# Retention in 128x32 column tiles accumulated in PSUM, and the score mask in four 64x64 tiles a slot

## The reference, cut to what matters

```python
# retention, 16 heads of 8 channels
q = l2_normalize(xn @ qw.T);  k = l2_normalize(xn @ kw.T);  v = xn @ vw.T
sim = einsum('bhnd,bhmd->bhnm', qh, kh) * scale
sim = sim * dmask            # gamma[h] ** (n - m) where n >= m, else 0
yh = einsum('bhnm,bhmd->bhnd', sim, vh)
x = x + (yh @ ow.T + ob)
...
# local attention, window 64
sim = where((i < j) | (i > j + WINDOW) | (j == -1), -big, sim)
attn = softmax(sim)
```

## Time and profile before

| what | us |
|---|---|
| time, median of 3 runs | 1068.89 (1068.8 to 1069.12) |
| time of the profiled execution | 1067.32 |
| span from its first to its last instruction | 1065.5 |
| outside the span (1067.32 - 1065.5) | 1.8 |

### The profile page before, as it was taken

One profiled execution on the slowest core, in us unless ns is written; L12 is line 12 of the kernel. 1 busy time (PEld: TensorE's weight loads), 2 busy tenths in 40 slices (PEclk: granted clock), 3 DMA queues, 4 the chain that ended last, 5 costly groups with the idle time before them and its releaser, 6 DMA issues.

```text
span 1065.5 us, 22792 instructions
## 1 busy us (share of the span) xinstructions
PE 964.0 (90%) x8404; PEld 660.6 (62%) x8404; DVE 752.1 (71%) x1225; ACT 693.1 (65%) x1347; POOL 619.8 (58%) x474
## 2 busy tenths in 40 slices
PE   1679899999999999999999969999999999999876
PEld 1347676685676766857767655756565656565552
DVE  5766676676767766767677676678787979696833
ACT  1354765847757658477576657777777768786643
POOL 4576566655755666558566655665665757575600
PEclk9989999999999999999999989999999999999997
DMA  9000000000000000000000000000000000000000
GB/s 293 1 1 1 1 2 2 2 1 0 0 1 0 0 0 0 0 0 0 0 0 0 1 1 1 2 2 21 0 20 0 20 0 20 0 20 0 21 21 10
DMA packets 20404, 12.31 MB, mean 12 GB/s; under 512 B 4578, under 2 KB 19596, under 8 KB 20236
## 3 DMA queue, kind: packets, MB, share of 16 engines
q1 hardware_dynamic: 15108, 10.49, 3.2%
q10 hardware_dynamic: 5256, 1.28, 0.6%
HBM read 9.67 MB, written 2.10 MB: 11 GB/s over the span
## 4 chain that ended last, share of the span: by engine, by line
PE 57%; DVE 15%; ACT 10%; POOL 8%; issue 7%; DMA 1%; DVEq 1%; ACTq 0%; SPq 0%; POOLq 0%
PE pQK L1140 6%; PE pS L1043 4%; PE pT L1054 4%; PE pS L1069 4%; PE pM L1086 4%; PE pT L1016 3%; PE pM L1210 3%; PE pS L1251 3%; PE pV L1106 3%; DVE m L720 3%; DVE xa L890 3%; PE pQK L1285 2%; DVE ss L710 2%; PE pS L1030 2%; PE pT L1242 2%
## 5 line engine op out<-in xcount | busy, mean ns | idle before, releaser
L367 POOL TENSOR_TENSOR rn<-rn,half_neg 128x16 f32<-128x16 f32 x64 | 187.5, 2929 | 5.3
L380 POOL TENSOR_TENSOR m<-m 128x1024 f32<-128x1024 f32 x64 | 150.9, 2358 | 0.0
L365 POOL TENSOR_SCALAR rn<-ss 128x16 f32<-128x16 f32 x64 | 16.5, 258 | 219.9 <-DVE ss L710 218.6
L730 DVE TENSOR_REDUCE mx<-pS 128x8 f32<-128x1024 f32 x64 | 78.1, 1220 | 74.4 <-PE pS L1043 74.4
L387 POOL TENSOR_TENSOR qkn<-m,rn 128x1024 f32<-128x1024 f32 x64 | 123.7, 1933 | 6.1 <-POOL m L380 2.0
L1140 PE MATMUL pQK<-wqkv,hT 128*128 128x512 f32 x256 | 124.2, 608 | 1.9 <-DVE m L720 1.9
L511 ACT ACTIVATE kT<-pT 128x512 f32<-128x512 f32 x64 | 38.0, 595 | 94.3 <-PE pT L1016 93.8
L551 ACT ACTIVATE sq<-pQK 128x1024 f32<-128x1024 f32 x64 | 65.4, 1021 | 29.9 <-PE pQK L1140 29.9
L710 DVE TENSOR_REDUCE ss<-sq 128x16 f32<-128x1024 f32 x64 | 77.4, 1210 | 7.0 <-ACT sq L551 6.9
L535 ACT ACTIVATE prT<-pT 128x1024 f32<-128x1024 f32 x64 | 65.4, 1022 | 25.5 <-PE pT L1054 24.4
L732 DVE TENSOR_TENSOR pr<-pS,mx 128x1024 f32<-128x1024 f32 x64 | 78.3, 1224 | 2.2
(11 more groups left out here) (172 smaller groups left out, 2356.8 us busy)
## 6 DMA issues: line engine op xcount, KB each, us to landing
x<-in_L_attn_x SPq DMA_DIRECT2D x4, 512.0 KB, 8.2
xs<-in_L_attn_x SPq DMA_DIRECT2D x8, 256.0 KB, 2.8
out<-aqkT SPq DMA_DIRECT2D x8, 256.0 KB, 2.3
wqkv<-in_L_ffn_wqkv SPq DMA_DIRECT2D x2, 768.0 KB, 10.4
tab<-in_k_tab SPq DMA_DIRECT2D x1, 1024.0 KB, 10.8
w<-in_L_ffn_w SPq DMA_DIRECT2D x2, 341.0 KB, 10.5
wo<-in_L_ffn_wo SPq DMA_DIRECT2D x2, 256.0 KB
cst<-in_k_cst ACTq DMA_DIRECT2D x1, 404.5 KB, 3.6
```

Source lines behind the costliest of these rows:

```text
L367: eng.tensor_tensor(rn[:, k % 2, :], rn[:, k % 2, :], half_neg[:, 0:2 * H], ALU.pow).then_inc(S["rn_done"], 1)
L380: eng.tensor_tensor(m1[:, k % 2, :], m1[:, k % 2, :], m2[:, k % 2, :], ALU.add).then_inc(S["add_done"], 1)
L730: eng.tensor_reduce(mx[:, :], sc, AX.X, ALU.max).then_inc(S["mx_done"], 1)
```

## The change

1. **Values** (`pe_block_values`): 16 matmuls of 128x32 weights by 32 columns a block, one for each chunk and residue j of the head in its group, each into a column tile of 32 PSUM partitions. They read the input itself, so the fourfold copy `xa4` goes. DVE spreads the 128 columns over 512 while it masks (L846 before; the output stays 512 elements).
2. **Sums** (`pe_block_sums`): ACT copies v into `avm` in 4 instructions with 32, 64, 96 and 128 rows; 4 matmuls of 128x32 weights by 128 columns, in four column tiles, give all chunks at once. DVE masks 128 columns in place of 512.
3. **State**: it is no longer added by DVE. PE adds it in PSUM, and POOL updates it once a step for the four blocks, at the end of its retention (`pool_state`).
4. **Output** (`pe_block_output`): 4 matmuls by 128 columns (state), 12 by 32 columns (sums of earlier chunks), 16 by 32 columns (`vx` with `sm`), all in column tiles of one bank `pY`, which holds four blocks. ACT copies it out once a step in place of 16 times.
5. **Order**: the projections run two blocks ahead in two banks (`qkv_banks`), and the scores of a block come after the next block's transposes.
6. **Mask** (`pe_scores`): four matmuls of 64x64 weights by 512 columns, one for each quarter of the array, in place of two of 128x128.

```diff
-            mask = mask16[:, 0 if is_first(step) else 1, :].unsqueeze(1).broadcast_to([P, 4, P])
-            for g in range(2):
-                eng.matmul(pS[:, g * 512:(g + 1) * 512], mask16[:, 2, :], mask, start=True, stop=False,
-                           skip_group_check=True)
+            for w in range(2):
+                for g in range(2):
+                    r = slice(64 * g, 64 * g + 64)
+                    kind = 2 if w else (0 if is_first(step) else 1)
+                    mask = mask16[r, kind * P:(kind + 1) * P].unsqueeze(1).broadcast_to([64, 4, P])
+                    eng.matmul(pS[64 * w:64 * w + 64, g * 512:(g + 1) * 512], mask16[r, 3 * P:3 * P + WIN], mask,
+                               start=True, stop=False, skip_group_check=True)
...
+        def pe_block_values(eng, t, b):
+            need(eng, A["vx"], 4 * t + b)
+            for c_ in range(NBL):
+                for j in range(NG):
+                    mm = eng.matmul(pT[BL * j:BL * j + BL, c_ * BL:(c_ + 1) * BL], xa[:, b, c_ * BL:(c_ + 1) * BL],
+                                    value_weights[:, :, j, :], start=True, stop=True)
+            mm.then_inc(A["vx_mm"], 1)
...
+        def pe_block_sums(eng, t, b):
+            if b == 0:
+                eng.wait_ge(LS["o_done"], 4 * t + 1)
+            need(eng, A["kvm"], 4 * t + b)
+            for g in range(NG):
+                cols = slice(BL * g, BL * g + BL)
+                mm = eng.matmul(pS[cols, 0:P].rearrange("p (c n) -> p c n", c=NBL), aqk[:, b % 2, 1, cols],
+                                avm[:, b % 2, :, cols], start=True, stop=True)
+            mm.then_inc(A["kv_mm"], 1)
...
+        def pe_block_output(eng, t, b):
+            n = 4 * t + b
+            need(eng, A["state"], t)
+            for g in range(NG):
+                rows = slice(BL * g, BL * g + BL)
+                eng.matmul(pY[rows, b * P:(b + 1) * P].rearrange("p (c n) -> p c n", c=NBL), state[:, b, :],
+                           qx[:, b % 2, :, g, :], start=True, stop=False, skip_group_check=True)
+            eng.wait_ge(A["kvm"], n + 1)
+            for c_ in range(1, NBL):
+                for g in range(NG):
+                    rows, col0 = slice(BL * g, BL * g + BL), b * P + c_ * BL
+                    eng.matmul(pY[rows, col0:col0 + BL], before[:, b, c_ - 1, :], qx[:, b % 2, c_, g, :], start=False,
+                               stop=False, skip_group_check=True)
+            eng.wait_ge(A["vx"], n + 1)
+            eng.wait_ge(A["sm"], n + 1)
+            for c_ in range(NBL):
+                for g in range(NG):
+                    rows, col0 = slice(BL * g, BL * g + BL), b * P + c_ * BL
+                    mm = eng.matmul(pY[rows, col0:col0 + BL], vx[:, b % 2, c_, rows], sm[:, b % 2, c_, g, :],
+                                    start=False, stop=True, skip_group_check=True)
+            mm.then_inc(A["y_mm"], 1)
...
         def dve_retention(eng, t, old):
             for k in range(NB + 1):
+                if k > 0:
+                    dve_block_scores(eng, t, k - 1)
                 if k < NB:
-                    if k < NB - 1:
-                        dve_retention_qk(eng, t, k + 1)
                     eng.wait_ge(A["vx_mm"], n + 1)
...
+                if k == 0:
+                    dve_retention_qk(eng, t, 1)
+                if k + 2 < NB:
+                    dve_retention_qk(eng, t, k + 2)
+                if k == NB - 1 and old:
+                    dve_ln(eng, old)
...
             need(eng, A["kv_mm"], n - 1)
-            eng.activation(av[:, b % 2, :], pV[:, 2 * P:3 * P], ACT.Copy).then_inc(A["v"], 1)
+            for c_ in range(NBL):
+                rows = slice(0, (c_ + 1) * BL)
+                copied = eng.activation(avm[rows, b % 2, c_, :], bank[rows, 2 * P:3 * P], ACT.Copy)
+            copied.then_inc(A["v"], 1)
...
+        def pool_state(eng, t):
+            eng.wait_ge(A["y_mm"], 4 * t + 4)
+            eng.tensor_tensor(state[:, :, :], state[:, :, :], state_decay.unsqueeze(2).broadcast_to([P, NB, BL]),
+                              ALU.mult).then_inc(A["faded"], 1)
+            eng.wait_ge(A["faded"], t + 1)
+            eng.tensor_tensor(state[:, :, :], state[:, :, :], before[:, :, NBL - 1, :], ALU.add).then_inc(A["state"], 1)
```

More of the change, by code:

```diff
@@ L51 @@
 C_END = C_SD + 1
+MASK_END = 3 * P + WIN
 def constants():
@@ L88, in constants @@
     before = (i[:WIN, None] <= i[None, :WIN])
+    first = np.concatenate([own, np.zeros_like(before)], 1)
     even = np.concatenate([own, before], 1)
     odd = np.concatenate([before, own], 1)
[L91 to L95, removed]
+    mask = np.where(np.concatenate([first, even, odd], 1), 0.0, MASKED).astype(f)
+    mask = np.concatenate([mask, np.eye(WIN, dtype=f)], 1)
+    mask = np.concatenate([mask, mask], 0)
     return cst, np.ascontiguousarray(tab), np.ascontiguousarray(mask)
@@ L600, in act_retention_project @@
             n = 4 * t + b
[L601 to L606, removed]
+            bank = qkv_banks[b % 2]
             eng.wait_ge(A["qkv_mm"], n + 1)
@@ L629, in act_retention @@
                         act_shift_residual(eng, old)
[L630 to L637, removed]
+                if k + 2 < NB:
+                    act_retention_project(eng, t, k + 2)
+            eng.wait_ge(A["y_mm"], 4 * t + 4)
+            eng.activation(ayT, pY, ACT.Copy).then_inc(A["yt"], 1)
         def act_block_ffn(eng, t):
@@ L872, in dve_block_scores @@
             eng.wait_ge(A["st_mm"], n + 1)
+            need(eng, A["y_mm"], n - 1)
             eng.tensor_tensor(sm[:, b % 2, :, :, :],
@@ L1218, in pe_retention_project @@
                 eng.wait_ge(LS["v_ev"], 2 * (4 * t + 4))
-            need(eng, A["qk"], 2 * n)
-            eng.matmul(pV[:, 0:3 * P], xa[:, b, :], aT[:, 0:3, :], start=True, stop=True).then_inc(A["qkv_mm"], 1)
+            need(eng, A["qk"], 2 * (n - 1))
+            eng.matmul(qkv_banks[b % 2][:, 0:3 * P], xa[:, b, :], aT[:, 0:3, :], start=True,
+                       stop=True).then_inc(A["qkv_mm"], 1)
         def pe_retention(eng, t, old):
@@ L1254, in pe_retention @@
-                if k == NB - 1:
-                    if old:
-                        eng.wait_ge(A["t_ev"], 4 * t + 4)
-                        pe_ln(eng, old)
-                    pe_block_scores(eng, t, k)
-                if k > 0:
-                    b = k - 1
-                    n = 4 * t + b
-                    eng.wait_ge(A["sm"], n + 1)
-                    eng.wait_ge(A["before"], n + 1)
-                    need(eng, A["yt"], NG * (n - 1))
-                    for c_ in range(NBL):
-                        cols = slice(512 + c_ * P, 512 + (c_ + 1) * P)
-                        eng.matmul(y_banks[b % 2][:, cols], vx[:, b % 2, c_, :], sm[:, b % 2, c_, :, :], start=True, stop=False)
-                        mm = eng.matmul(y_banks[b % 2][:, cols], before[:, b % 2, c_ - 1, :] if c_ else state[:, b, :],
-                                        qx[:, b % 2, c_, :, :], start=False, stop=True)
-                    mm.then_inc(A["y_mm"], 1)
@@ L1272, in pe_retention @@
-                if k < NB - 1:
-                    pe_block_scores(eng, t, k)
+                if k == 0:
+                    pe_retention_project(eng, t, 1)
+                if k > 0:
+                    pe_block_scores(eng, t, k - 1)
+                if k + 2 < NB:
+                    pe_retention_project(eng, t, k + 2)
+                if k == NB - 1 and old:
+                    eng.wait_ge(A["t_ev"], 4 * t + 4)
+                    pe_ln(eng, old)
+                if k < NB:
+                    pe_block_values(eng, t, k)
+                    pe_block_sums(eng, t, k)
```

139 lines of the change are left out of this document (59 added, 80 removed).

## The result

The changed kernel takes 1042.71 us (median), the kernel before took 1068.85 us on the same chip: 0.9747 of it, with a 95% interval of 0.9733 to 0.976. It is faster, by 26.1 us where I had forecast 66; 1042.7 lies 2.7 us above my range. (One further execution of the changed kernel took 1561.88 us at a mean granted clock of 0.718; it is not in the ratio, and the others took 1040.27 to 1043.18.) The profiled execution has a span of 1040.4 us at a mean granted clock of 0.953, against 1065.5 us at 0.985 before.

A forecast was written before the change was run, and what follows sets the result against it. PE's own stream was taken to set the pace in layer 0. Retention 59, mask 8 + 2.4, clock -4 gave 66 us; 1065.5 - 66 + 1.8 = 1001.3, median predicted 1002; forecast 994 to 1013, range 982 to 1040.

The forecast's parts named there:

- What small tiles cost: PE's small matmuls in retention: 16 take 0.40 us, 12 take 0.30; a block takes 3.5 us in place of 5.9.
- Retention, by the waits: Layer 0's retention, followed through PE's waits: ends 6.8 us a body earlier, with PE idle 3.4 us before block 1.
- Behind retention, and the mask: Two PE waits behind retention go, 0.6 us a body; the mask gains 8 us in layer 0, 2.4 in layer 1.
- The two waits: PE's waits behind retention, 0.36 us for the last ACT copy and 0.23 for `x1`: both go, 0.6 us.
- 7.4 x 8 = 59 us: Retention's whole gain in layer 0: 7.4 us in each of eight bodies, 59 us.
- The clock: PE's new idle 3.4 us lowers the clock in less than a third of the bodies: 4 us lost.
- my third rival: The clock falls in every body, 6.8 us at half clock behind each idle stretch: 27 us lost, 1025; chance 0.15.
- What would show it: Signs: layer 0 body about 62.5 us, 16 small matmuls 0.3 to 0.5, wait for q and k about 3.4, mask 0.25.
- if the clock dips through layer 0: One of three signs, named beforehand, that the prediction is wrong: the clock dipping through layer 0; no size given.

The follow-up runs named there:

- e1: The changed kernel with PE's hardware loop in layer 0 written out as six bodies: 1011.73 us, 0.9479 of the kernel before.
- e3: The kernel before with the new mask alone (four 64x64 matmuls a slot): 1058.21 us, 0.9909 of the kernel before.
- e2: The kernel before with PE's hardware loop in layer 0 written out: 1068.6 us against 1068.23.
- e5: The kernel before with PE's layer 0 loop making three passes of two bodies each: 1075.36 us, 1.0063 of the kernel before.
- e9: The changed kernel, loop kept, with all four blocks' values as whole 128x128 matmuls and block 1's keys early as in e6: 1005.99 us.
- e10: As e9, but with whole values in blocks 0 and 1 alone: 1028.0 us, 0.961 of the kernel before.
- e6: The changed kernel, PE's loop written out, block 1's q and k before block 0's masks, block 0's scores before block 1's transposes: 1000.12 us.
- e12: The kernel of e6 with small matmuls ordered tile by tile in place of round the four column tiles: 1010.61 us.

## Why the prediction was wrong

By its own steps:

- **What small tiles cost: right mechanism, price too high.** I took 0.40 us for 16, from bounds of 0.27 and 1.08; they take 0.28 from start to start. By the Trainium skill's page TensorEngine Tiling (Array Packing), section Instruction Overhead, it would have been 0.54 us (the prediction's estimate), and no such tiles would have been chosen. The rows disagree.
- **Retention, by the waits: right.** PE idles 3.14 us ahead of block 1 (forecast 3.4), block 1's transposes start 5.5 us behind block 0's (5.7), and PE meets no wait for POOL in later blocks. In body 1 retention takes 18.6 us from block 0's transposes to the turn, for 17.8 forecast and 24.6 before. Gaps of 0.54 and 0.66 us ("issue") among the small matmuls are what I had not counted there; e1 has 4.7 us of them at L1287 over the program.
- **Behind retention, and the mask: right in sum.** The two waits are gone, and the mask gives 10.0 us for 10.4 (e3). A slot gains 0.28 us in e3's chain for the 0.33 that I took, and half of it at the scores. Body 1 shrinks from 70.8 to 63.5 us, 7.3, where my forecast for a body was 8.4.
- **The step that failed: a term is missing.** "What small tiles cost" and "Retention, by the waits" priced PE's instructions by their durations and waits only, and "7.4 x 8 = 59 us" took all eight bodies as equal. The instructions also have to be loaded, a cost that stands in no term of the sum and in no rival. The body's stream grew from 1285 to 1872 records, past a limit between 1684 and 1780, and each of the five jumps back then costs 3.65 to 3.94 us: 18.9 us, shown by e1 (without), e2 (control), e5 (before, with), and e9 and e10 (either side of the limit). The slow clock behind the stalls is the likely rest of e1's 31.0, 12.1 us, within the 17.6 that it can cost at most. Three quarters of the 40.7 us by which I missed is this.
- **The clock: right mechanism, wrong size.** I put 4 us on it, less than a third of the bodies. Even without the stalls six of the eight bodies have a stretch of slow clock behind the 3.1 us wait (row 396.27 of e1). With it the program has 30.5 us more of slow clock than before, worth up to 15.2. That is nearly my third rival, which gave 1025; it took 6.8 us for each stretch, and five of the six are 3.4 us long. The slow clock and the gaps among the small matmuls are what is known for the 9.7 us that are left; how they divide was not measured apart.
- **What would show it.** The wait for q and k and the starts about 0.01 us apart came as named. The groups of 16 are just below the 0.3 us that I named, and the mask takes 0.34 us in e3 for 0.25. The period of the loop's bodies stayed at 70.7 for 62.5, and "if the clock dips through layer 0", my sign of being wrong, came true.

**Open.** Body 1 has the same 3.14 us wait as the loop's bodies and keeps its clock; e5 has two like stalls and a fall behind one. That fewer or shorter idle times keep the clock up in e6 and e12 is argued from their rows, not shown apart. The limit is known between two counts for one program. e5 changes PE's code alone, so the count is one of PE's stream; whether it goes by instructions, by bytes or by whole packets was not tried. Why gaps of 0.2 to 1.1 us arise among dense small matmuls was not tried either; that e1, whose code arrives in a straight line, has 5.8 us of them, and e9, whose code stays loaded, none, speaks for code loading. So does e12: its code is as long and in a straight line too, its small matmuls ask for it more slowly, and it has none. That e10 has only 0.8 speaks against.

## What to carry to other kernels

Splitting matmuls into small tiles multiplies instructions, so count the instructions of one pass of a hardware loop as well as their time; a body that no longer stays loaded pays a stall at every jump back, which shows as "issue" idle ahead of the loop's first instruction and as more packets on the instruction queue. When a loop's bodies and a written-out body of the same work differ in time, look there first; writing the loop out, or making the body shorter by dearer instructions, wins it back. And a re-ordering that opens one idle stretch of some 3 us in a busy TensorE stream is paid twice here, by the wait and, in six of e1's eight bodies, by the slower clock behind it.

## What was not expected of the hardware

- A jump back to code that is not loaded costs PE 3.5 to 4.0 us (2.9 to 3.1 in e5), and no more for a longer body; the 69 packets that come while PE runs in a straight line (e1) bring no such stall.
- Sixteen float32 matmuls of 128x32 weights by 32 columns are 32 records. From the first record's start to the last one's they take 0.26 us round four column tiles (e6), 8.5 ns a record, and 0.70 us tile by tile (e12), 22.6 ns a record. The Trainium skill's page TensorE: Matmul & The Clock Gate, section "Wait — 56ns, not 53.3ns?", has a floor of about 25 ns from start to start; for records in different column tiles these runs go far below it, and tile by tile, with 22.6 ns, a little below.
- Exchanging two loops in the source, with the same instructions, is worth 9 to 10.5 us of 1000.
